# Two-layer transformer kernel on Trainium2: another order of the work in the main attention

## The reference

```python
q_mid = rmsnorm(hidden_states @ q_a_w.T, q_a_ln_w)
q = (q_mid @ q_b_w.T).reshape(b, s, H, D_Q).transpose(0, 2, 1, 3)      # H = 16, D_Q = 128 + 64
kv_a = hidden_states @ kv_a_w.T                                         # 64 latents, 16 x 64 rotary keys
q_pe = apply_rope(q_pe, cos, sin)
k_pe = apply_rope(k_pe, cos, sin)
scores = jnp.einsum('bhqd,bhkd->bhqk', qf, kf) * scale
probs = jax.nn.softmax(scores.astype(jnp.float32), axis=-1)
ctx = jnp.einsum('bhqk,bhkd->bhqd', probs, v)
main_out = ctx.transpose(0, 2, 1, 3).reshape(b, s, H * D_V) @ o_w.T
```

## Time and profile before

| | |
|---|---|
| median of three runs | 1569.32 us (1567.0 to 1569.37) |
| the profiled execution | 1566.81 us |
| its span | 1565.0 us |
| busy: PE, PE's weight loads, VectorE | 1426.5, 841.9, 926.7 us |
| busy: ScalarE, GpSimd | 747.3, 548.9 us |
| mean granted clock of TensorE | 0.952 |

### The profile page before, as it was taken

The page is one execution under the profiler, slowest core; times in us unless marked ns, Lnnn a source line. Parts: engine busy times, 40 slices in busy tenths (PEclk is TensorE's granted clock), DMA queues, the critical chain, the costliest instruction groups (busy, mean ns, idle before and its releaser), DMA issues. The chain is left out here.

```text
span 1565.0 us, 20565 instructions
## 1 busy us (share of the span) xinstructions
PE 1426.5 (91%) x7287; PEld 841.9 (54%) x7350; DVE 926.7 (59%) x1719; ACT 747.3 (48%) x1368; POOL 548.9 (35%) x454
## 2 busy tenths in 40 slices
PE   6889999899999999999999968899579999879998
PEld 3533333355455555454545546788434444468887
DVE  5588776456666666666666344444458787544445
ACT  3457776654545454545453324233235555435553
POOL 4260162155565655656566522233200000101210
PEclk9979999999999999999999968899789999959999
DMA  7980000000000000000001011110076000101110
GB/s 292 179 114 1 2 21 7 1 1 0 1 1 0 1 1 1 1 1 1 1 1 42 0 41 39 36 55 27 1 168 93 1 1 1 50 21 41 41 41 27
DMA packets 20442, 53.04 MB, mean 34 GB/s; under 512 B 4630, under 2 KB 7464, under 8 KB 19123
## 3 DMA queue, kind: packets, MB, share of 16 engines
q1 hardware_dynamic: 20341, 51.73, 13.6%
HBM read 42.28 MB, written 8.39 MB: 32 GB/s over the span
## 5 line engine op out<-in xcount | busy, mean ns | idle before, releaser
L1631 POOL TENSOR_TENSOR Ps<-Ps,Pb 128x512 f32<-128x512 f32 x192 | 245.3, 1291 | 161.4 <-ACT Pb L1614 161.4
L1614 ACT ACTIVATE Pb<-bank 128x512 f32<-128x512 f32 x256 | 152.9, 597 | 287.5 <-PE bank L1603 235.0
L1575 DVE TENSOR_REDUCE mp<-bank 128x1 f32<-128x512 f32 x256 | 171.7, 687 | 141.6 <-PE bank L1568 139.7
L1062 DVE TENSOR_REDUCE mp<-bank 128x2 f32<-128x1024 f32 x128 | 153.6, 1222 | 48.4 <-PE bank L1054 48.0
L1121 ACT ACTIVATE Pb<-bank 128x512 f32<-128x512 f32 x256 | 133.2, 600 | 39.7 <-PE bank L1104 39.3
L1568 PE MATMUL bank<-qk1h,qk0h 128*128 128x512 f32 x256 | 135.7, 541 | 7.7 <-DVE mp L1575 7.7
L1600 PE MATMUL bank<-qk0h,qk1h 128*128 128x512 f32 x256 | 124.3, 486 | 6.1 <-DVE mrow L996 6.1
L1645 PE MATMUL bank<-Pb,kvx 128*64 128x512 f32 x512 | 124.0, 605 | 1.0 <-ACT Pb L1614 0.7
L1246 ACT ACTIVATE Pb<-bank 128x512 f32<-128x512 f32 x192 | 84.7, 489 | 80.2 <-PE bank L1233 57.4
L1214 DVE TENSOR_REDUCE mp<-bank 128x1 f32<-128x512 f32 (+1 forms) x192 | 97.8, 552 | 17.6 <-PE bank L1204 11.5
L1602 PE MATMUL bank<-qk0h,qk1l 128*128 128x512 f32 x256 | 101.2, 396 | 0.0
(11 more groups left out here) (341 smaller groups left out, 3265.5 us busy)
## 6 DMA issues: line engine op xcount, KB each, us to landing
wr<-wf SPq DMA_DIRECT2D x25, 256.0 KB, 2.6
wraw<-wf SPq DMA_DIRECT2D x8, 768.0 KB, 4.1
scratch<-stgr SPq DMA_DIRECT2D x4, 1024.0 KB, 3.9
scratch<-stg SPq DMA_DIRECT2D x4, 768.0 KB, 7.0
owT<-owT SPq DMA_DIRECT2D x1, 2048.0 KB, 9.9
qbn<-qbn SPq DMA_DIRECT2D x1, 1536.0 KB, 14.9
qstr<-scratch SPq DMA_DIRECT2D x12, 128.0 KB
kstr<-scratch SPq DMA_DIRECT2D x12, 128.0 KB
```

What stands on the lines that cost most here:

```text
L1062: e.tensor_reduce(mp[:, w % 3, :, j, kh], wide[slot][:], AX, ALU.max).then_inc(ring_ok, 1)
L1575: e.tensor_reduce(mp[:, u % 3, hd, j, kh:kh + 1], bank[b][:, 0:c], AX, ALU.max).then_inc(mp_ok[2], 1)
L1614: e.activation(Pbm[n % NPBM][:], bank[b][:], ACT.Exp, scale=SC0).then_inc(exp_ok[2], 1)
L1631: e.tensor_tensor(Ps[z][:], first, Pbm[n % NPBM][:], ALU.add).then_inc(sum_ok, 1)
```

## The change

Only the order of the main attention changes, and what goes with it; no instruction is added or taken away.

1. The `prep` parts start at steps 1, 5, 9, 13, 17 and 21 of the 32 of a pair of units, so that every `product` stands at an odd step, right before the run of `pv` where there is one. A step of pause stands between `turn` and `high`.
2. `den` and both `project`s stand right behind a run of `pv` (where several things are due at one step, `pv` now goes first).
3. VectorE's additions are an entry of their own, `add`, one step behind their `project`.
4. The maxima of the next unit begin one step earlier in odd units and end one step earlier in all; `neg` stands at step 10 (before: 12) and `tr` and `row` at step 12 (before: 14).
5. `ctx` and `cadd` of units 0 and 1 get other steps.

```diff
     def run_due():
-        for d in [d for d in due if d[0] <= n]:
+        for d in sorted((d for d in due if d[0] <= n), key=lambda d: d[1][0][0] != "pv"):
...
-        begin, last_max = (0, nk) if ahead == 2 else (3 * (u % 2), nk - 5)
+        begin, last_max = (0, nk) if ahead == 2 else (2 * (u % 2), nk - 6)
...
-PREP_TIMES = (0, 1, 2, None, 3, 4, 5, None, 6, 7, 8, None, 9, 10, 11, None, 12, 13, 14, None, 15, 16, 17, None, 18, 19)
+PRODUCT_AT = ((R0, 1), (Q0, 5), (R1, 9), (R2, 13), (Q1, 17), (R3, 21))
+AFTER = {"rope": ("product", "swap", "turn", "", "high", "low"), "lat": ("product", "high", "low")}
+PREP = [tuple((part, AFTER[part[0]][t - at]) for part, at in PRODUCT_AT if 0 <= t - at < len(AFTER[part[0]]))
+        for t in range(32)]
...
-    chunks = []
-    out = [(kind, i) for i in range(NT) for kind in ("ctx", "cadd")]
+    out = {u: {k + d: (("ctx", "cadd")[d], 4 * u + i) for i, k in enumerate(ks) for d in range(2)}
+           for u, ks in ((0, (0, 4, 8, 10)), (1, (0, 2, 4, 6)))}
...
     def evac(u):
-        return [(0, [("den", u)]), (1, [("recip", u)]), (4, [("project", u, 0)]), (6, [("project", u, 1)])]
-    order = attention_order(16, 2, False, 2, 1, (2, 3, -4, -2), at_begin, at_step, evac, lead=False)
+        return [(1, [("den", u)]), (2, [("recip", u)]), (5, [("project", u, 0)]), (6, [("add", u, 0)]),
+                (9, [("project", u, 1)]), (10, [("add", u, 1)])]
+    order = attention_order(16, 2, False, 2, 1, (2, 3, -6, -4), at_begin, at_step, evac, lead=False)
...
-    B6_KINDS = ("row", "project", "cadd")
+    B6_KINDS = ("row", "add", "cadd")
...
-            elif s[0] == "project":
+            elif s[0] == "add":
                 dve_add_out(e, s)
```

More of the change, by code:

```diff
@@ L111, in attention_order @@
     return order
-PREP_TIMES = (0, 1, 2, None, 3, 4, 5, None, 6, 7, 8, None, 9, 10, 11, None, 12, 13, 14, None, 15, 16, 17, None, 18, 19)
+R0, R1, R2, R3, Q0, Q1 = ("rope", 0), ("rope", 1), ("rope", 2), ("rope", 3), ("lat", 0), ("lat", 1)
+PRODUCT_AT = ((R0, 1), (Q0, 5), (R1, 9), (R2, 13), (Q1, 17), (R3, 21))
+AFTER = {"rope": ("product", "swap", "turn", "", "high", "low"), "lat": ("product", "high", "low")}
+PREP = [tuple((part, AFTER[part[0]][t - at]) for part, at in PRODUCT_AT if 0 <= t - at < len(AFTER[part[0]]))
+        for t in range(32)]
 def main_order():
-    chunks = []
-    out = [(kind, i) for i in range(NT) for kind in ("ctx", "cadd")]
+    out = {u: {k + d: (("ctx", "cadd")[d], 4 * u + i) for i, k in enumerate(ks) for d in range(2)}
+           for u, ks in ((0, (0, 4, 8, 10)), (1, (0, 2, 4, 6)))}
     def at_begin(u):
-        if u % 2 == 0 and u // 2 + 1 < 8:
-            chunks.extend(("prep", u // 2 + 1, i) if i is not None else None for i in PREP_TIMES)
         return [("keys", 1)] if u == 0 else []
     def at_step(u, k):
-        now = [c for c in chunks[:1] if chunks.pop(0) is not None]
-        if (u == 0 and 1 <= k < 13) or (u == 1 and 2 <= k < 6):
-            now.append(out.pop(0))
+        now, t = [], 16 * (u % 2) + k
+        if u // 2 + 1 < 8 and PREP[t]:
+            now.append(("prep", u // 2 + 1, t))
+        if k in out.get(u, ()):
+            now.append(out[u][k])
         return now
     def evac(u):
-        return [(0, [("den", u)]), (1, [("recip", u)]), (4, [("project", u, 0)]), (6, [("project", u, 1)])]
-    order = attention_order(16, 2, False, 2, 1, (2, 3, -4, -2), at_begin, at_step, evac, lead=False)
+        return [(1, [("den", u)]), (2, [("recip", u)]), (5, [("project", u, 0)]), (6, [("add", u, 0)]),
+                (9, [("project", u, 1)]), (10, [("add", u, 1)])]
+    order = attention_order(16, 2, False, 2, 1, (2, 3, -6, -4), at_begin, at_step, evac, lead=False)
     order.insert(1 + max(i for i, s in enumerate(order) if s[0] == "st"), ("norm", 0))
@@ L215, in causal_order @@
     return attention_order(32, 1, True, 4, 2, (2, 2, 0, 2), lambda u: [], at_step, lambda u: [(0, [("evac", u)])])
[L219 to L227, removed]
 FIRST = (R0, R1, R2, Q0, Q1, R3)
@@ L530, in dve_stats @@
                 elif j == 0:
-                    e.wait_ge(b6_ok[2], B6M["project", 14 + half, 1] + 1)
+                    e.wait_ge(b6_ok[2], B6M["add", 14 + half, 1] + 1)
                 e.bn_stats(st6[:, i, :], x[:, i, :]).then_inc(st_ok, 1)
@@ L1638, in pe_pvm @@
             if u >= 2:
-                e.wait_ge(b6_ok[2], B6M["project", u - 2, 1] + 1)
+                e.wait_ge(b6_ok[2], B6M["add", u - 2, 1] + 1)
             else:
@@ L1701, in dve_add_out @@
         e.wait_ge(pr_mm, NO_M[s])
-        e.wait_ge(b6_ok[2], (B6M["project", u - 2, q] if u >= 2 else B6M["cadd", 4 * u + 2 * q + 1]) + 1)
+        e.wait_ge(b6_ok[2], (B6M["add", u - 2, q] if u >= 2 else B6M["cadd", 4 * u + 2 * q + 1]) + 1)
         for hd, b in ((0, 6), (1, 4 + u % 2)):
```

## The result

The changed kernel takes **1669.8 us** (median of four runs, 1666.73 to 1674.85), the kernel before beside it on the same chip 1568.16 (1565.61 to 1569.37): a ratio of 1.0654, 95% interval 1.0618 to 1.0689. The forecast was 1624 with a range of 1600 to 1650: the direction was right, and of 101.6 us only 55 were foreseen.

What follows compares the result with a forecast made beforehand. PE was taken as the bound, busy 91%. Waits of 12.4 us per pair instead of 3.3 gave +55 over six pairs; first +6, last -1, joins -5: +55 on 1566.8, 1622; median 2.5 higher, 1624 us, range 1600 to 1650.

Steps and rivals of the forecast that it cites:

- The `swap` on ScalarE: Scores wait for the exponential behind a `swap` at R0, R1 and R2: 0.8, 1.8 and 2.0, together 4.6 us per pair.
- The maxima on VectorE: PE waits for maxima because VectorE's work comes in one piece after a long PE run: together 7.3 us per pair.
- The six places: Waits for maxima: even units 1.8 to 2.2 and 0.8; odd units 1.6, 1.2, 1.0 and 0.5 us.
- The clock: Rival: new waits in the main attention drop PE to half clock, once per unit with `prep`: +24, so 1648 us; chance 0.12.
- the sign of being wrong: The prediction would be wrong if, among other signs, the granted clock in the main attention fell below 1.00.
- The wait for `tr`: The transpose on PE waits for VectorE's additions: 0.1 us per pair.
- The joins: `den` or `project` right behind `pv` saves 0.6 us per pair, 5 in all (0 to 16); `product` beside `pv` gains nothing.
- The `row` waits: With `tr` two steps earlier, PE's waits for `row` of about 0.7 and 0.5 us per pair go.
- GpSimd, "nothing": GpSimd's 28 sums per pair stay unchanged and only `den` asks for the last, now later: no cost.
- First and last pair: First pair of units +6 us (0 to 9); last pair, without `prep` and partly without maxima, -1.
- The rival that the `swap` alone would bite: Waits for maxima stay at 2.1 us per pair while only `swap` waits are added: 1591 us; chance 0.10.
- the rings absorb the step: Rival: PE's queue runs on through the new places, old waits vanish and joins add: 1537 us; chance 0.04.

Runs made afterwards that it cites:

- e6: The changed kernel with each `swap` moved into the step of its `product`, ahead of the run of `pv`: 1633.36 us, ratio 1.0436.
- e9: The changed kernel with the `low` of R0 at step 10 instead of 6 and that of R2 at 21 instead of 18: 1617.62 us.
- e2: The kernel before with only the change's maxima, `neg` and `tr`: 1565.46 us, ratio 0.9999.
- e4: The changed kernel without six of GpSimd's seven sums for each head of a unit: 1624.31 us, ratio 1.0383.
- e5: The kernel before without six of GpSimd's seven sums for each head of a unit: 1560.79 us, ratio 0.997.

## Why the prediction was right and wrong

- **The `swap` on ScalarE: right.** Forecast 0.8, 1.8 and 2.0, measured 0.99, 1.88 and 2.04, and e6 takes away all three.
- **The maxima on VectorE: the places right, the size wrong, and this is the step that failed.** The six places are those of the forecast. The four small ones measure 3.8 without the slow clock (0.86, 1.22, 1.30, 0.41; e9 has 0.68 + 0.18 for the join at even 4.1), where 3.5 were forecast. The two large ones are 3.75 and 3.51 instead of 2.0 and 1.6. What failed is the price of VectorE's work between the run on PE and the next maximum: "The rows have a first half of 1.54 and a second of 0.68; I took these", the 1.4 for the `low` of R2, and the 0.3 for `recip`. The second half of R0's `low` took 1.66 (+1.0), `recip` 0.8 more than its row, the `low` of R2 3.2 (+1.8): 3.6 together, and 3.75 + 3.51 exceed the forecast's 3.6 by 3.7. (The six terms of the forecast add up to 7.1, not to its 7.3.)

  The rows were no accident. In the kernel before R0's `low` takes 1.54 + 0.68, R2's 0.69 + 0.68 and `recip`'s second operation in an even unit 0.17, in each of the six middle pairs alike. They are prices of the old order. There GpSimd has a pause from 561.83 to 564.02, in which the second half of R0's `low` (562.40) and `recip` fall, and another behind 589.21, in which R2's `low` falls; the `low` of R1 falls on three sums. GpSimd and VectorE in the trace of the kernel before:

```profile
560.56 1.27 POOL L1631 TENSOR_TENSOR Ps<-Ps,Pb 128x512 f32<-128x512 f32 x1 [0.43 <-ACT Pb L1614]
564.02 2.51 POOL L1631 TENSOR_TENSOR Ps<-Ps,Pb 128x512 f32<-128x512 f32 x2 [2.19 <-ACT Pb L1614]
...
578.89 4.20 POOL L1631 TENSOR_TENSOR Ps<-Ps,Pb 128x512 f32<-128x512 f32 x3
...
587.93 1.28 POOL L1631 TENSOR_TENSOR Ps<-Ps,Pb 128x512 f32<-128x512 f32 x1
```
```profile
580.33 1.62 DVE L1496 TENSOR_TENSOR qk1l<-Rt,qk1h 64x512 fp32r<-64x512 f32 x1 [1.38 <-ACT qk1h L1475]
581.97 1.67 DVE L1498 TENSOR_TENSOR qk1l<-Rt,qk1h 64x512 fp32r<-64x512 f32 x1
...
589.36 0.69 DVE L1496 TENSOR_TENSOR qk0l<-Rt,qk0h 64x512 fp32r<-64x512 f32 x1 [3.92 <-ACT qk0h L1475]
590.07 0.68 DVE L1498 TENSOR_TENSOR qk0l<-Rt,qk0h 64x512 fp32r<-64x512 f32 x1
```

  In the new order R0's `low` and `recip` (609.31 to 613.70) meet sums from 609.04 to 610.33 and from 610.74 to 613.67, and R2's `low` (646.81 to 650.04) those that start at 646.53 and 648.23. What the trace of before did show is how far the price of one instruction moves from place to place. VectorE's instructions there that write `qk1l`, 350 to 900 (duration ns min/median/max):

```profile
L1496 DVE TENSOR_TENSOR qk1l<-Rt,qk1h x13: 1271/1552/1628, 348.8 to 809.4; 64x512 fp32r<-64x512 f32 x13
L1498 DVE TENSOR_TENSOR qk1l<-Rt,qk1h x13: 682/1674/1684, 350.1 to 811.1; 64x512 fp32r<-64x512 f32 x13
```

  The 0.68 is R0's, the 1.67 R1's. The rule of the Trainium skill ("SBUF — State Buffer", section "SBUF: two separate sides"), that VectorE with two SBUF inputs and GpSimd shut each other out for a whole instruction, agrees with this: the `low`s and the second operation of `recip` and the last of `neg`, which have two such inputs, are stretched, and those with an input from a bank are not. The conversion in `neg`, with one input from SBUF, is longer too (0.53 at 668.86, 0.17 without sums), which the rule in these words does not cover. I let rows outvote it. But I had also applied it to the `low` of R0 alone: the 5 us that the prediction put on it would have made 1629, and R2's `low` and `recip` were left out of that sum too.
- **The clock: a rival with a chance of 0.12, and it came on top.** The falls came as that rival named them, one in each unit, and with them the sign of being wrong that the prediction ended on, a granted clock below 1.00. At even 4.1 they cost 0.94 (1.62 against e9's 0.68) and at odd 0.1 1.05 (1.69 against 0.64): 2.0 per pair and 12 in all, less than the 1.7 each of the earlier trace rows, since a part falls on waits that were there anyway. I had set it as another case, though each wait added to the forecast made it likelier.
- **The wait for `tr`: missed.** GpSimd's sums stretch `neg` (1.19 for 0.17) and the `low` of R3, VectorE's additions come late, and `tr` waits for them, 1.2 instead of 0.1. Without sums, or with the earlier `swap`, it is 0.
- **The joins: right in sum, not in kind.** `pv` with `project` behind it saves 0.18, four times per pair, 0.72 for the 0.6; `product` with `pv`, and `pv` with `den`, cost just what they cost apart. So float32 beside `pv` gains nothing, as forecast.
- **The `row` waits are gone, the DMA queues cost nothing: right.** e2 shows that in the old order the gain of the `row` waits is taken back by maxima.
- **GpSimd, "nothing": wrong.** By the path that the prediction looked at it is right: in the six middle pairs no wait of PE is ended by GpSimd. By the other, through VectorE, the sums cost 42 us of the new order (e4) and 5 of the old (e5). And VectorE's additions, of which the prediction held that one step later costs nothing, are what `tr` waits for (1.2 for the 0.1).
- **First and last pair.** The first pair of units grew from 81.8 to 94.0 us, by 12.2 where 6 were forecast, by the same causes; the last fell by 1.0, as forecast. Behind the last score the program took 649.9 us instead of 656.1; over the kernels of this study it took 648.7 to 656.1, with no tie to their order that I can see, and this stays open. These 6 us less are luck for the forecast: the part that the change touches was missed by more than the total.
- **The miss by its terms.** A middle pair waits 7.4 us longer than forecast: 3.7 for the two `low`s and `recip`, 2.0 for the clock, 1.1 for `tr`, and the rest in small ones.

The sum of profiled executions, 99.9: six pairs 94.7 (forecast 51, joins taken off), first 12.2 (5.4 with its joins), last -1.0 (-1), what follows -6.1 (0). The rival that the `swap` alone would bite is refuted: the waits for maxima came in full beside it. That the rings absorb the step is refuted too.

## What to carry over

Before an instruction of one engine is put behind a long run of another, ask what stood behind it until now and covered it; two moves that cost 3 and 35 us alone cost 102 together here, when one takes away the cover of the other. Look at all occurrences of an instruction in the trace, by place. Where they differ (here 0.68 and 1.67 for the same one) the price depends on a neighbour, and even a row that repeats in every pair is a price of the old order: take the neighbours that the instruction will have (here GpSimd's sums), or the longest duration as the bound. Where new waits of several us come close to each other, put the slow clock into the sum and not beside it.

## What the hardware showed that I had not expected

- A VectorE instruction with two SBUF inputs beside GpSimd's sums takes up to a sum (1.29) longer, at both sizes that occur here: 64 x 512 goes from 0.68 to 1.54 to 1.67, and 128 x 8 from 0.17 to 1.00 and 1.19. Two in a row can both pay. A reduction of a bank (0.68) and a subtraction with one input from a bank (0.67) pay nothing.
- Not every long wait of PE is followed by a slow clock. It was, behind 0.55 and 1.62 us of work in 3.5 and 3.4; behind a stretch with 0.15 in 3.40 (up to 650.80) the clock stayed at 1.00. The first two stretches end where the clock fell and the third was laid around a wait, so they are not cut alike; what makes the difference isn't settled here.
- `project` right behind `pv` saves 0.18, while entering `pv` from a float32 `product` saves nothing against entering it from a float32r score.
